# Graph attention with a three-layer FFN: the turn of E moved off TensorE, the first norm moved to ScalarE, gamma and beta folded into W1 and b1, and the opening reordered

## The reference

```
h = relu(norm(x))                        # norm: (x - mean) / sqrt(var + eps)
for l in 0..2:
    si, sj = h @ attn_w[l, :256], h @ attn_w[l, 256:]
    s  = leaky_0.2(si[:, None] + sj[None, :] + attn_b[l]), -inf where no edge
    h  = norm(h + softmax(s) @ h) * g1[l] + beta1[l]
    h  = norm(h + gelu(h @ W1[l] + b1[l]) @ W2[l] + b2[l]) * g2[l] + beta2[l]
out = x + h
```

## Time and profile before

| | |
|---|---|
| median of 3 runs | 1242.52 us (1242.37 to 1242.93) |
| the profiled execution | 1241.6 us, its span 1239.8 us |
| TensorE matmul busy | 1196.4 us |
| VectorE, ScalarE, GpSimd busy | 1075.9, 920.0, 677.4 us |
| granted TensorE clock, mean | 0.998 |
| DMA | 100.57 MB, 26.3% of 16 engines |

### The profile page before, as it was taken

One profiled execution on the slowest core, in us unless ns is written; L12 is line 12 of the kernel. 1 busy time (PEld: TensorE's weight loads), 2 busy tenths in 40 slices (PEclk: granted clock), 3 DMA queues, 4 the chain that ended last, 5 costly groups with the idle time before them and its releaser, 6 DMA issues.

```text
span 1239.8 us, 23072 instructions
## 1 busy us (share of the span) xinstructions
PE 1196.4 (97%) x7509; PEld 1082.8 (87%) x7509; DVE 1075.9 (87%) x3568; ACT 920.0 (74%) x1754; POOL 677.4 (55%) x648
## 2 busy tenths in 40 slices
PE   2699999999999999999999999999999999999997
PEld 1589999998999999999999999999999999999996
DVE  5899889999998888899998888899989988888865
ACT  3786887678877776778778767777887777677752
POOL 1354455456755554456666545554666455545564
PEclk9999999999999999999999999999999999999999
DMA  7122322233332111222432122122432321122221
GB/s 256 38 77 73 99 70 60 77 94 112 103 103 88 50 44 52 85 71 85 129 114 92 43 59 70 44 69 78 125 115 80 100 60 43 44 69 61 78 89 48
DMA packets 109620, 100.57 MB, mean 81 GB/s; under 512 B 12952, under 2 KB 95932, under 8 KB 109500
## 3 DMA queue, kind: packets, MB, share of 16 engines
q1 hardware_dynamic: 109500, 99.10, 26.3%
HBM read 66.47 MB, written 32.60 MB: 80 GB/s over the span
## 4 chain that ended last, share of the span: by engine, by line
PE 95%; DVE 3%; SPq 1%; DMA 1%; issue 0%; POOL 0%; ACT 0%; DVEq 0%; POOLq 0%
PE acc L1073 44%; PE hbank L1058 42%; PE mix L1087 7%; PE mix L1112 2%; DMA adji<-in_adj_dram 1%; DVE xs L757 0%; DVE junk L694 0%; DVE st L603 0%; DVE st L764 0%; SPq L313 0%; PE util L1104 0%; SPq L332 0%; DVE sc L729 0%; POOL rstd L467 0%; DVE hid_lo L615 0%
## 5 line engine op out<-in xcount | busy, mean ns | idle before, releaser
L1073 PE MATMUL acc<-w2hi,hid_hi 128*128 128x256 f32 x1536 | 442.2, 288 | 0.0
L1073 PE MATMUL acc<-w2hi,hid_lo 128*128 128x256 f32 x1536 | 434.5, 283 | 0.0
L1073 PE MATMUL acc<-w2lo,hid_hi 128*128 128x256 f32 x1536 | 434.4, 283 | 0.0
L912 ACT ACTIVATE hbank<-hbank,vec 128x512 f32<-128x512 f32 x384 | 255.4, 665 | 178.1 <-PE hbank L1058 167.0
L1058 PE MATMUL hbank<-ht_hi,w1hi 128*128 128x512 f32 x768 | 305.7, 398 | 3.6 <-DVE hid_lo L615 2.0
L1058 PE MATMUL hbank<-ht_lo,w1hi 128*128 128x512 f32 x768 | 300.7, 392 | 0.0
L1073 PEld LDWEIGHTS acc<-w2lo,hid_hi 128*128 128x128 f32 x1536 | 294.0, 191 | 6.9
L1073 PEld LDWEIGHTS acc<-w2hi,hid_hi 128*128 128x128 f32 x1536 | 293.9, 191 | 6.9
L1058 PE MATMUL hbank<-ht_hi,w1lo 128*128 128x512 f32 x768 | 299.3, 390 | 0.0
L615 DVE TENSOR_TENSOR hid_lo<-hbank,hid_hi 128x512 fp32r<-128x512 f32 x384 | 259.9, 677 | 39.4 <-ACT hid_hi L918 39.4
L1073 PEld LDWEIGHTS acc<-w2hi,hid_lo 128*128 128x128 f32 x1536 | 293.9, 191 | 0.0
(11 more groups left out here) (80 smaller groups left out, 1708.4 us busy)
## 6 DMA issues: line engine op xcount, KB each, us to landing
z_dram<-tz SPq DMA_DIRECT2D x46, 512.0 KB, 2.6
zt<-z_dram SPq DMA_DIRECT2D x184, 128.0 KB, 2.8
sj_bc<-sj_dram SPq DMA_DIRECT2D x47, 256.0 KB, 3.9
xraw<-in_x_dram SPq DMA_DIRECT2D x16, 512.0 KB, 4.1
out_dram<-xout SPq DMA_DIRECT2D x32, 256.0 KB, 3.0
xres<-in_x_dram SPq DMA_DIRECT2D x15, 512.0 KB, 5.0
xout<-in_L_gnn_W_dram SPq DMA_DIRECT2D x10, 512.0 KB, 5.5
adji<-in_adj_dram SPq DMA_DIRECT2D x16, 256.0 KB, 3.5
```

The lines of the kernel that those rows point to most:

```text
L912: act.activation(hbank[k % HB][:], hbank[k % HB][:], ACT.Gelu, bias=b1c(i.l, c)).then_inc(gelu_n, 1)
L1073: mm = pe.matmul(to, v[:, k % HID, of_g], w[:, i.l, c], start=c == 0 and n == 0 and g % HG == 0, stop=c == C - 1 and n == 2, skip_group_ch ...
```

## The change

1. **Fold of gamma and beta.** The high and low parts of W1 are made from g1 times W1, row by row. TensorE makes W1-transposed times beta1 (`beta_rows`, eight one-column matmuls for each half of a W1), VectorE adds the sums to b1 (`beta_sums`). `h_out` is gone: `h_high` and `h_low` read `zt` in SBUF (items 0 and 1: `util`).
2. **First norm on ScalarE.** `norm1` becomes four activations with a bias of minus mean times rstd, which `shift1` makes on VectorE.
3. **E turned by VectorE.** From item 2 on `turn_e` turns 32 x 32 blocks of `sc` into a new tile `te`; one write to DRAM (`send_e`, 256 KB) and four reads (`move_e`, 64 KB each) bring them to their places, and ScalarE's `et_out` copies `te` to `ET`. Both the turn's output and the copy's input have a step of four floats. Items 0 and 1 are turned by TensorE into `util`.
4. **Early loads.** Inputs and masks of items 1 and 2 have tiles of their own (`EARLY` = 2: `hb`, `zt`, and `tz` for the masks), and the weights come ahead of the bias rows.
5. **Other orders** in the opening and in the slot of every engine.

The core of the diff:

```diff
-EARLY = 1
+EARLY = 2
+            def send_e(i):
+                sp.wait_ge(te_n, moved(i.q))
+                wait(sp, et_in, MOVES * (moved(i.q) - 1))
+                sp.dma_start(e_dram, te[:].rearrange("p b t g -> p (b t g)")).then_inc(e_sent, 16)
+            def move_e(i):
+                sp.wait_ge(e_sent, 16 * moved(i.q))
+                for b in range(NQ):
+                    sp.dma_start(te[b * QD:(b + 1) * QD].rearrange("p a t g -> p a (t g)"),
+                                 e_dram.rearrange("(a p) (b f) -> b p a f", a=NQ, b=NQ)[b]).then_inc(et_in, 16)
...
             def slot(s):                      # SP
+                send_z(b), move_z(b), send_e(a), move_e(a), send_out(o, 1), load_weights(s + 7),
+                send_out(o, 0), load_xres(t), send_sj(d), load_sj(d), load_xraw(n), load_adj(n)
...
             def slot(s):                      # GpSimd
+                h_beta(f, 1), h_gamma(b, 1), h_beta(b, 0), make_rstd("2", t), x_gamma(t, 0), x_beta(t, 0),
+                x_gamma(t, 1), x_beta(t, 1), make_rstd("0", p), add_input(t), make_rstd("1", a), h_gamma(a, 0)
...
+            def turn_e(i):
+                dve.wait_ge(exp_n, GG * (i.q + 1))
+                dve.wait_ge(eto_n, i.q)
+                dve.transpose(te[:].rearrange("p b i g -> p b g i"), sc[:].rearrange("p g (b j) -> p b g j", j=QD)).then_inc(te_n, 1)
-            def norm1(i):
+            def shift1(i):
                 dve.wait_ge(rstd_n["1"], i.q + 1)
-                    dve.tensor_scalar(x_of(i)[:, g], x_of(i)[:, g], mv["1"][:, g, 0:1], rstd["1"][:, g:g + 1],
-                                      ALU.subtract, ALU.mult).then_inc(z1_n, 1)
+                dve.scalar_tensor_tensor(out=nmr1[:], in0=mv["1"][:, :, 0], scalar=-1.0, in1=rstd["1"][:],
+                                         op0=ALU.mult, op1=ALU.mult).then_inc(nmr1_n, 1)
...
             def slot(s):                      # VectorE
+                residual(t, 1), low(f, 1), minus_max(a), moments2(t), low(f, 2), turn_e(a), penalty(p),
+                split_weights(s + 5), norm2(t, 0), beta_sums(s + 5), low(f, 3), input_moments(p), norm2(t, 1),
+                low(f, 4), low(f, 5), h_low(b, 0), low(f, 6), h_low(b, 1), j_dots(d), attend(a, 0),
+                input_shift(p), attend(a, 1), low(f, 7), moments1(a), i_dots(d), shift1(a), low(b, 0),
+                masked(d), residual(f, 0), turn_z(a)
...
+            def norm1(i):
+                act.wait_ge(nmr1_n, i.q + 1)
+                for g in range(GG):
+                    act.activation(x_of(i)[:, g], x_of(i)[:, g], ACT.Identity, bias=nmr1[:, g:g + 1],
+                                   scale=rstd["1"][:, g:g + 1]).then_inc(z1_n, 1)
             def et_out(i):
+                wait(act, agg_n, 2 * i.q)
+                if i.q >= BY_PE:
+                    act.wait_ge(et_in, MOVES * moved(i.q))
+                    act.copy(ET[:], te[:].rearrange("p a i g -> p g (a i)")).then_inc(eto_n, 1)
...
             def slot(s):                      # ScalarE; gh is gelu_high
+                gh(f, 2), exps(a), gh(f, 3), gh(f, 4), gh(f, 5), h_high(b, 0), gh(f, 6), h_high(b, 1),
+                et_out(a), round_weights(s + 6), gh(f, 7), gh(b, 0), first_x(p), gh(b, 1), norm1(a), leaky(d)
...
             def slot(s):                      # TensorE
+                ffn1(f, 3), ffn2(f, 0), ffn1(f, 4), ffn2(f, 1), ffn2(f, 2), ffn1(f, 5), ffn1(f, 6),
+                ffn2(f, 3), ffn2(f, 4), ffn1(f, 7), aggregate(a), ffn1(b, 0), ffn1(b, 1),
+                ffn2(f, 5), ffn2(f, 6), ffn2(f, 7), ffn1(b, 2), beta_rows(s + 6)
```

More of the change, by code:

```diff
@@ L272, in wait_e_turned @@
         def wait_e_turned(eng, q):
-            wait(eng, et_n, q + 1)
+            if q < BY_PE:
+                wait(eng, et_n, q + 1)
+            else:
+                eng.wait_ge(te_n, moved(q))
         def wait_z_turned(eng, q):
@@ L556, in slot @@
                     add_input(t, 1)
-                if n and n.l == 0:
-                    make_rstd("0", n.g)
+                if a:
+                    make_rstd("1", a.q)
+                    h_gamma(a, 0)
                 if s == ITEMS - 2:
@@ L832, in slot @@
                     masked(d)
-                if b:
-                    low(b, 1)
+                if f:
+                    residual(f, 0)
+                if a:
+                    turn_z(a)
             i0, i1, i2, i3 = (item(q) for q in range(0, 4))
             input_moments(i0)
+            turn_vectors()
+            penalty(i0)
             input_shift(i0)
-            penalty(i0)
-            turn_vectors()
+            penalty(i1)
             j_dots(i0)
+            i_dots(i0)
+            masked(i0)
@@ L842, in _ @@
+            minus_max(i0)
             input_moments(i1)
-            i_dots(i0)
+            input_shift(i1)
+            attend(i0, 0)
+            attend(i0, 1)
+            input_moments(i2)
+            moments1(i0)
             split_weights(0)
-            input_shift(i1)
-            masked(i0)
-            penalty(i1)
-            minus_max(i0)
+            beta_sums(0)
+            shift1(i0)
             j_dots(i1)
-            input_moments(i2)
+            split_weights(1)
+            split_weights(2)
@@ L876, in _ @@
             low(i0, 2)
-            penalty(i3)
-            input_shift(i3)
+            split_weights(4)
             low(i0, 3)
+            shift1(i1)
+            turn_e(i2)
+            beta_sums(4)
+            low(i0, 4)
+            h_low(i1, 0)
+            low(i0, 5)
+            j_dots(i3)
+            h_low(i1, 1)
+            low(i0, 6)
+            split_weights(5)
             attend(i2, 0)
-            low(i0, 4)
+            low(i0, 7)
             attend(i2, 1)
-            h_low(i1, 0)
@@ L884, in _ @@
             moments1(i2)
-            j_dots(i3)
-            low(i0, 5)
-            low(i0, 6)
-            h_low(i1, 1)
-            low(i0, 7)
+            residual(i0, 0)
+            masked(i3)
+            shift1(i2)
             i_dots(i3)
-            norm1(i2)
-            masked(i3)
-            split_weights(4)
+            beta_sums(5)
+            turn_z(i2)
             low(i1, 0)
-            turn_z(i2)
-            low(i1, 1)
             for s in range(1, ITEMS + 3):
@@ L1107, in e_turn, with beta_rows @@
             def e_turn(i):
-                wait(pe, y1_n, GG * (i.q - 1) + HG)
-                turned = mix[0][:].rearrange("p g d -> p (g d)")
+                wait_util_read()
+                read["e"] += 1
                 for g in range(GG):
                     pe.wait_ge(exp_n, GG * i.q + g + 1)
-                    mm = pe.transpose(turned[:, g * P:(g + 1) * P], sc[:, g], ident[:])
+                    mm = pe.transpose(util[:, g * P:(g + 1) * P], sc[:, g], ident[:])
                 mm.then_inc(et_n, 1)
+            def beta_rows(n):
+                if 0 <= n < len(halves) and halves[n][1] == 0:
+                    l, _, h = halves[n]
+                    pe.wait_ge(*half_arrived(n))
+                    if n == 0:
+                        pe.wait_ge(vec_ready, 1)
+                    wait_util_read()
+                    read["b"] += 1
+                    for c in range(C):
+                        mm = pe.matmul(util[:, c:c + 1], half_staged(n)[:, c * P:(c + 1) * P], beta1c(l, h),
+                                       start=c == 0, stop=True, skip_group_check=True)
+                    mm.then_inc(wbeta_n, 1)
             def slot(s):
```

432 lines of the change are left out of this document (247 added, 185 removed).

## The result

The changed kernel takes **1257.03 us** (median of 4 runs, 1255.92 to 1258.7), the kernel before 1242.44 beside it (4 runs, 1242.2 to 1242.93). The ratio is 1.0119, 95% interval 1.0105 to 1.0132: **slower by 1.2%**. The forecast was 1231, range 1217 to 1244, with 0.11 for slower. The profiled execution has a span of 1254.1 us against 1239.8. VectorE's share of the span went from 87% to 94%, and the chain, 95% on TensorE before, now runs over VectorE for a third of its length.

The account below looks back on a forecast made before the run. TensorE, busy for 97% of the span, was taken as the bound. 19.8 - 1 - 5 - 8.4 + 2.9 + 3 = 11.3 us off the median of 1242.5 gave about 1231, range 1217 to 1244.

Parts of the forecast that it names:

- All this I cost at nothing: Reordered SP transfers and GpSimd's new order, with the same operations at 14.1 us an item: no cost.
- the low parts of h come from SBUF instead of PSUM, same size, no change: VectorE's low parts of h in a slot: reading SBUF instead of PSUM changes their time by nothing.
- The walk: New slot stepped through with old-trace durations: period 24.2 us, the chain between aggregates holding with 0.2 to 0.3 spare.
- E off TensorE, 19.8 us: Four transposes of E leave TensorE's list: 0.44 us a slot, 19.8 us won in 45 slots.
- E through DRAM, hidden: E's write, reads and copy finish before the aggregate wants it at 38.2, by 0 to 0.9 us.
- rival D: E comes late by DRAM, aggregate waits behind the copy of te: slower, about 1271 us; chance 0.10.
- Turn 0.9, copy 0.86: E's turn on VectorE 0.9 us and copy of te on ScalarE 0.86 us, with a step of four floats.
- Rival C: Chain between aggregates binds every slot if turn and copy cost 1.24 and 1.0: 1241 us; chance 0.17.
- `beta_rows` 1 us in two slots: Eight one-column matmuls on TensorE for each half of a W1: 1 us for the two in slots.
- Slots with input, 0.7 more: first_x delays the norm, TensorE waits about 0.7 us in each of twelve input slots: 8.4 us.
- rival B: Margins wider than walked, input slots cost what they did, opening gives most of its stall: 1221 us; chance 0.20.
- Opening, 3 us won: Earlier mask load lets full slots start at 75 to 76 instead of 78.85: 3 us won.

Follow-up runs that it names:

- run 1: Changed kernel with GpSimd's h_beta, x_gamma and x_beta on 32 of 256 columns: 1241.2 us, 0.9996 of the kernel before.
- run 11: run 9 with add_input's halves apart, the first after masked, the second after the next minus_max: 1232.14 us, 0.9912 of the kernel before.
- run 3: Changed kernel with every item's E turned by TensorE into util again: 1261.75 us, 1.0153 of the kernel before.
- run 10: run 9 with E of all items turned by TensorE again: 1277.7 us, 1.0285 of the kernel before.
- run 5: Changed kernel with contiguous te and GpSimd's h_beta, x_gamma, x_beta on 32 of 256 columns: 1234.33 us, 0.9937 of the kernel before.
- run 7: Changed kernel with contiguous te, GpSimd's slot reordered behind minus_max, norm2 and j_dots, norm2's halves together: 1268.34 us, 1.0209 of the kernel before.
- run 9: run 7 with add_input behind rstd1 instead of ahead of h_beta, h_gamma and rstd1: 1249.27 us, 1.0068 of the kernel before.
- run 6: Changed kernel with GpSimd waiting for minus_max before the slot's h_beta(f, 1): 1268.44 us, 1.0213 of the kernel before.

## Why the prediction was wrong

The step that failed is "**All this I cost at nothing**", said of GpSimd's new order, together with "the low parts of h come from SBUF instead of PSUM, same size, no change" and the bare list of VectorE's durations. The walk took each operation at its mean in the old trace, as if that belonged to the operation. It belongs to the pair: what GpSimd runs at the time is part of it. Before, GpSimd did both multiplications of `h_gamma` together (2.53 us) once both halves of `residual` were done, and was idle up to 9.1 us ahead of them, so `minus_max` fell clear of them:

```profile
425.82 2.53 POOL L487 TENSOR_TENSOR hb<-xs,ln_rows 128x512 f32<-128x512 f32 x2 [9.09 <-DVE xs L629]
...
425.78 0.16 DVE L740 SCALAR_TENSOR_TENSOR negm<-below 128x4 f32<-128x4 f32 x1
```

After, four such operations follow one another for 5 us, over `minus_max` at each item, and `x_gamma`, `x_beta` lie over `norm2` and `ht_lo`. The low parts of h do take the same time from SBUF when nothing stands beside them (0.69 in run 1), so that term's size was right and its condition wrong. The waits are 133.6 us of VectorE's time. Forecast was 0.3 us less for VectorE in a slot of 24.2; it got 100.7 / 48 = 2.1 more in one of 25.0. Between the first and the last aggregate of the full slots the changed kernel needs 24.6 us more than run 11 (92.08 to 1194.04 against 93.02 to 1170.36), and some 8 of them lie at one place of TensorE's list, behind `low(f, 2)`.

Point by point:

- **E off TensorE, 19.8 us**: right. Runs 3 and 10 show 0.43 to 0.44 a slot, so following the Trainium skill's rule that the prediction quotes, a 128 x 128 transpose to TensorE, would lose here. (The 390 ns quoted with it are that page's figure for a bf16 block; these blocks are fp32.) TensorE's own list is 24.31 to 24.33 (runs 1, 5, 7, 9, 11), against the 24.2 of the walk.
- **E through DRAM, hidden**: right in most slots. The transfers land earlier than taken, 2.1 and 1.9 us, but turn and copy are longer, and in nine slots TensorE waits for `ET`, 3.0 us in all. The prediction named such waits in plain slots as the sign of rival D; at that size they don't carry the loss. That the kernel is slower, as D said, came of another cause.
- **Turn 0.9, copy 0.86**: undersized. The step made them 1.10 and 1.13, the copy beyond its upper bound of 1.0. Rival C's worry was right in direction, but it is the smaller part: 9 us in the changed kernel, 6 once the waits are gone.
- **`beta_rows` 1 us in two slots**: 26.05 - 24.33 = 1.72 each, so 3.4 in all. The forecast had eight matmuls for each half; the trace has sixteen in 1.84 us:

```profile
127.62 1.84 PE L1231 MATMUL util<-vec,xout 128*128 128x1 f32 x16
```

- **Slots with input, 0.7 more**: the changed kernel has 25.5 against the 24.9 forecast. Run 11 has 24.5, only 0.2 above plain. So `first_x` does not bind as the walk had it: the full durations it added overlap in part, as rival B said, and the excess was the port's and the step's.
- **Opening, 3 us won**: 78.70 - 77.06 = 1.6 (the prediction's 78.85 for the first full slot is read from the chain; its first matmul starts at 78.70). `ffn1(i0, 3)` comes at 45.2, close to the 46 of the walk; the rest is lost after it. The opening also depends on the granted clock, which the walk took as full. Runs 9 and 11 have the same opening; in the traced execution of run 9 the clock was 1.00 from 27 to 47 us and the first full slot starts at 76.65, in that of run 11 it was 0.50 (1.2 GHz), sixteen one-column matmuls took 3.41 us instead of 1.89, and the slot starts at 78.80. The changed kernel's trace has 1.00 there.
- **The sum.** Forecast for the slots was a gain of 8.3 us; they lost some 16. The difference of 24 is about what runs 5 and 11 take away (22.7 and 24.9). Without these two faults the change does nearly what was forecast, 1232.14 against 1231. That this fits so closely is in part luck: in the trace of run 11 the opening wins nothing instead of 3, `beta_rows` costs 3.4 instead of 1, and slots with input cost far less than the 8.4 walked.

The number was outside the range because no rival held this mechanism. Rows could have warned. Dot products (0.512 us) and `masked` (0.419) of the kernel before are 0.474 and 0.387 after, with the same operands and another order on GpSimd: part of their price was, it seems, already a wait. In run 9, where `add_input` lies over `masked`, it is 0.421 again. The 419 against 280 ns from which the strided price was scaled were thus no clean pair.

How much each of the four collisions costs by itself was not measured. They were taken away together, and run 6, which took one, moved the others.

## What to carry to other kernels

A duration in a profile is that of an operation among its neighbours. If GpSimd works on SBUF, mark each VectorE instruction with two SBUF operands and each `tensor_scalar`, however small, and lay GpSimd's work beside those that read PSUM or have one input; a reordering of GpSimd needs a price of its own while VectorE is near full. When a small instruction takes an odd time, look at what on the other engine ends at the same moment before calling the engine overloaded. And an operation that can wait for a load does not stand ahead of work that another engine is waiting for.

## What the runs showed that I had not expected

- An instruction on four elements a partition took 1.15 us on average instead of 0.16, and counted as busy. A share of 94% for VectorE held more than a tenth of waiting (133.6 of 1176.6 us).
- A step of four floats on one side makes a 128x512 blocked transpose on VectorE 1.10 instead of 0.70 us and a 128x512 copy on ScalarE 1.13 instead of 0.62: a factor of 1.6 to 1.8.
- With the same work on each engine and the same order on VectorE, an order of GpSimd's instructions alone moved the kernel from 1268 to 1232 us (runs 7 and 11).
- The same opening ended 2.15 us later where TensorE's granted clock was 0.50 from 27 to 47 us (run 11) than where it was 1.00 (run 9); that is most of what the opening was to win. What decides between the two is open.
